# A three-layer graph convolution on one core: how many columns of each step are fetched row by row, where they land, and how SyncE and ScalarE issue them

## What is computed

```python
def _sage_conv(x, src, dst, Wl, bl, Wr):
    agg = jax.ops.segment_max(x[src], dst, num_segments=x.shape[0])
    agg = jnp.where(jnp.isfinite(agg), agg, 0.0)
    return agg @ Wl + bl + x @ Wr
h = jax.nn.leaky_relu(_sage_conv(h, src, dst, Wl1, bl1, Wr1), NEG_SLOPE)   # and twice more
x = x + h
```

## Time and profile before

| | |
|---|---|
| median of 3 runs | 6052.55 us (6050.76 to 6064.11) |
| the profiled execution, its own time | 6050.56 us |
| its span in the profile | 6048.9 us |
| GpSimd busy | 4524.8 us, 75% |
| VectorE busy | 2893.5 us, 48% |
| TensorE busy | 732.5 us, 12% |
| ScalarE busy | 225.4 us, 4% (DMA issues are not counted) |
| mean DMA rate | 180 GB/s |

### The profile page before, as it was taken

How to read it: one execution, slowest core, us unless ns; L and a number is a source line. 1 busy time by engine, 2 the same in 40 slices (tenths; PEclk the granted TensorE clock), 3 DMA queues, 4 the chain that set the end, 5 groups by cost and what they waited for, 6 DMA issues and landing times.

```text
span 6048.9 us, 53349 instructions
## 1 busy us (share of the span) xinstructions
PE 732.5 (12%) x2214; PEld 411.8 (7%) x2214; DVE 2893.5 (48%) x3638; ACT 225.4 (4%) x664; POOL 4524.8 (75%) x4793
## 2 busy tenths in 40 slices
PE   1111111111100311111111110040010000100003
PEld 0000000000000200000000000030000000000002
DVE  5333333333333555555555555565555555555556
ACT  1000000000000100000000000010000000000001
POOL 6777777777777777777777777767777777777776
PEclk7555555555555655555555555575555555555556
DMA  4333333333333566666666666666666666666665
GB/s 141 108 111 107 108 108 109 110 108 108 108 108 107 171 216 218 218 216 220 216 218 218 216 219 214 215 206 219 217 220 215 218 218 216 220 215 218 215 216 175
DMA packets 461123, 1089.10 MB, mean 180 GB/s; under 512 B 116295, under 2 KB 181740, under 8 KB 461068
## 3 DMA queue, kind: packets, MB, share of 16 engines
q0 software_dynamic: 203520, 519.10, 30.6%
q1 hardware_dynamic: 220508, 544.04, 24.8%
q10 hardware_dynamic: 37040, 25.45, 1.5%
HBM read 555.08 MB, written 533.07 MB: 180 GB/s over the span
## 4 chain that ended last, share of the span: by engine, by line
POOL 49%; issue 17%; DMA 1%; POOLq 1%; DVE 0%; PE 0%; DVEq 0%
POOL ring L448 47%; POOL ring L475 2%; POOLq L444 0%; DMA ring<-running_max_log,end_row 0%; POOLq L441 0%; DMA patch<-running_max_log,patch_row 0%; DMA ring<-features,stage 0%; DMA running_max_log<-patch 0%; POOL patch L465 0%; DVE z_sum L902 0%; DVE agg L894 0%; POOLq L455 0%; POOLq L443 0%; DMA features<-h_out 0%; DVE patch L873 0%
## 5 line engine op out<-in xcount | busy, mean ns | idle before, releaser
L448 POOL DMA_INDIRECT ring<-features,stage x4611 | 4360.0, 946 | 1432.2 <-issue 1383.7
L792 DVE TENSOR_TENSOR ring<-banks,ring 128x1024 f32<-128x1024 f32 (+1 forms) x1173 | 1227.4, 1046 | 2954.0 <-DMA ring<-features,stage 2918.9
L758 DVE TENSOR_TENSOR banks<-ring,banks 128x1024 f32<-128x1024 f32 (+1 forms) x1173 | 1232.1, 1050 | 37.5
L975 PE MATMUL banks<-wr,h_turned 128*128 128x256 f32 (+1 forms) x490 | 220.7, 596 | 3623.4 <-ACT h_turned L1109 3623.4
L975 PEld LDWEIGHTS banks<-wr,h_turned 128*128 128x128 f32 x490 | 127.2, 320 | 3687.4 <-ACT h_turned L1109 3678.6
L991 PE MATMUL banks<-dst_low,own 128*128 128x394 bf16 x200 | 100.4, 502 | 976.0 <-DVE own L734 976.0
L475 POOL DMA_INDIRECT ring<-running_max_log,end_row x147 | 142.9, 972 | 65.6 <-issue 43.9
L1109 ACT ACTIVATE h_turned<-banks 128x256 f32<-128x256 f32 (+1 forms) x147 | 51.8, 353 | 3128.6 <-issue 2664.1
L739 DVE COPY stage<-edges 128x8 int32 (+1 forms) x588 | 119.4, 203 | 88.0 <-DVE banks L758 32.8
L977 PE MATMUL banks<-b,ones 1*128 1x256 f32 (+1 forms) x294 | 157.6, 637 | 0.0
L1048 PE MATMUL banks<-wl,agg 128*128 128x256 f32 (+1 forms) x490 | 110.7, 369 | 1.2 <-DVE agg L894 0.9
(11 more groups left out here) (114 smaller groups left out, 523.4 us busy)
## 6 DMA issues: line engine op xcount, KB each, us to landing
running_max_log<-ring SPq DMA_DIRECT2D x782, 512.0 KB, 3.1
running_max_log<-ring SPq DMA_DIRECT2D x391, 256.0 KB, 2.2
ring<-features ACTq DMA_DIRECT2D x4752, 1.0 KB
ring<-features,stage POOLq DMA_INDIRECT x4611, 3.2
ring<-features SPq DMA_DIRECT2D x3888, 1.0 KB
ring<-features ACTq DMA_DIRECT2D x2376, 0.5 KB
ring<-features SPq DMA_DIRECT2D x1944, 0.5 KB
h_in<-features ACTq DMA_DIRECT2D x98, 128.0 KB, 2.5
```

The source lines that it names most:

```text
L448: pool.indirect_dma_start(ring[0:rows, c * w:(c + 1) * w], None, tables[l], bass.IndirectOffsetOnAxis(ap=stage[0:rows, b, u:u + 1].bitcast ...
L758: dve.tensor_tensor(sum_ps[:, 0:CHAINS * w].rearrange("p (h f) -> p h f", h=CHAINS), group(g - 1).rearrange("p (h f) -> p h f", h=CHAINS), ...
L792: dve.tensor_tensor(group(g), sum_ps[:, 0:CHAINS * w], group(g), ALU.max).then_inc(turn, 1)
L975: pe.matmul(mm_ps[p][:, 0:n], h_turned[p][:, c, :], wr_sb[l][:, c, :], start=(c == 0), stop=False)
```

## The change

- GpSimd gathers 54 columns a step, all of 128 rows, and none of column 54. SyncE and ScalarE fetch 128 rows each (`FETCHED_COLS` 2), into one of two buffers, `fetched[0]` and `fetched[1]`, in turn, and no longer into `ring`.
- VectorE's last maximum of a step becomes two, of half the width each: the first takes the two gathered columns from `ring`, the second the two fetched ones from `fetched`; the waits for the rows stand between them.
- Because there are two buffers, the rows of step `i` may be fetched once step `i - 2` is scanned: both queues wait for `block_scanned` of `i * BLOCKS`, and no longer for a group of the same step nor for a store.
- A TENSOR_LOAD takes 32 words (`AT_ONCE`) on both queues. SyncE does it ahead of the wait for the block, then waits, stores the whole block of 8 columns with one DMA, and issues 32 rows behind it, in blocks 0 to 3. ScalarE issues four portions of 32; in layers 1 and 2 the four pieces of `keep_pair` stand between the portions (`step_of_rows`), in layer 0 behind them all.
- The loops on VectorE, ScalarE and SyncE have a body of two steps, since the buffer must be known to the instruction; step 0 stands ahead of them. GpSimd's loop keeps a body of one step.
- The last, short step is stored group by group as before.

```diff
-SYNC_ROWS, SYNC_AT_ONCE = 72, 8
-ACT_AT_ONCE = 11
-ROWS = 160
+FETCHED_COLS = 2
+SYNC_ROWS = 128
+AT_ONCE = 32
...
+    ROWS = FETCHED_COLS * P
...
-        return width(b, last) - (b == BLOCKS - 1 and not last)
+        return width(b, last) - (FETCHED_COLS if b == BLOCKS - 1 and not last else 0)
...
+        fetched = [sb(f"fetched{k}", [P, FETCHED_COLS * F_MAX]) for k in range(2)]
...
-                            rows = 2 * P - ROWS if c == RING_COLS - 2 and not last else P
                             pool.indirect_dma_start(
-                                ring[0:rows, c * w:(c + 1) * w], None, tables[l],
+                                ring[:, c * w:(c + 1) * w], None, tables[l],
...
-                        dve.tensor_tensor(group(g), sum_ps[:, 0:CHAINS * w], group(g), ALU.max).then_inc(turn, 1)
+                        if g == GROUPS - 1:
+                            gathered = (CHAINS - FETCHED_COLS) * w
+                            dve.tensor_tensor(group(g)[:, 0:gathered], sum_ps[:, 0:gathered], group(g)[:, 0:gathered],
+                                              ALU.max).then_inc(turn, 1)
+                            dve.wait_ge(act_rows_landed[turn_of], FETCHED[1])
+                            dve.sem_inc(act_rows_landed[turn_of], -FETCHED[1])
+                            dve.wait_ge(sync_rows_landed[turn_of], FETCHED[0])
+                            dve.sem_inc(sync_rows_landed[turn_of], -FETCHED[0])
+                            dve.tensor_tensor(group(g)[:, gathered:CHAINS * w], sum_ps[:, gathered:CHAINS * w],
+                                              fetched[turn_of][:, 0:FETCHED_COLS * w], ALU.max).then_inc(turn, 1)
...
+                def rows_open(i):
+
+                    if isinstance(i, int) and i == 0:
                         act.wait_ge(rows_placed, len(widths))
                     else:
-                        act.wait_ge(logged[BLOCKS - 1], i * (DMA * STORES_OF[BLOCKS - 1]) + LOGGED[BLOCKS - 1] * l)
+                        act.wait_ge(block_scanned, i * BLOCKS + SIGNED * l)
...
+                def step_of_rows(i, pair, turn_of):
+
+                    rows_open(i)
+                    if pair and l:
+                        for p in range(2):
+                            fetch_rows(i, turn_of, range(2 * p, 2 * p + 1))
+                            keep_turned(i, p, True)
+                            fetch_rows(i, turn_of, range(2 * p + 1, 2 * p + 2))
+                            keep_own(i, p)
+                    else:
+                        fetch_rows(i, turn_of, range(ACT_PORTIONS))
+                        if pair:
+                            keep_pair(i, 2)
...
+                    elif not last:
+                        sp.wait_ge(block_scanned, i * BLOCKS + SIGNED * l)
                     for b in used_blocks(last):
 
                         c, columns = b * BLOCK_COLS, width(b, last)
-                        if columns > CHAINS:
+                        fetches = not last and b < SYNC_PORTIONS
+                        if fetches:
+                            places = row_places(0, mybir.EngineType.SP, i, b * AT_ONCE, AT_ONCE, w)
+                        if last and columns > CHAINS:
                             sp.wait_ge(group_scanned, i * BLOCKS + (FIRSTS * l + b + 1))
...
                         sp.wait_ge(block_scanned, i * BLOCKS + (SIGNED * l + BLOCKS + b + 1))
-                        at = columns - CHAINS
-                        sp.dma_start(log_block(l, i, b, at, CHAINS), ring[:, (c + at) * w:(c + columns) * w]
+                        at = columns - CHAINS if last else 0
+                        sp.dma_start(log_block(l, i, b, at, columns - at), ring[:, (c + at) * w:(c + columns) * w]
                                      ).then_inc(logged[b], DMA)
-                        if not last and (BLOCK_GROUPS * b + 1) * SYNC_AT_ONCE < SYNC_ROWS:
-                            fetch_rows(i, BLOCK_GROUPS * b + 1)
+                        if fetches:
+                            fetch_rows(places, turn_of, b * AT_ONCE)
...
-                with sp.Fori(1, STEPS - 1) as i:
-                    log_step(i, False)
+                with sp.Fori(0, STEPS // 2 - 1) as i:
+                    log_step(i * 2 + 1, False, 1)
+                    log_step(i * 2 + 2, False, 0)
```

More of the change, by code:

```diff
@@ L23 @@
 BLOCK_GROUPS = BLOCK_COLS // CHAINS
-TURNS = 2 * GROUPS + 1
+TURNS = 2 * GROUPS + 2
 STORES = 5
@@ L307, in run_neighbours, with lists_of @@
             return pairs
[L309 to L316, removed]
+        def lists_of(edges_src):
+            return [(row_list[:, k * P:(k + 1) * P],
+                     bass.AP(edges_src.tensor, (CHAINS - 1 - k) * P * RUN + GROUPS - 1, [[GROUPS, STEPS - 1], [RUN, P]]))
+                    for k in range(FETCHED_COLS)]
         def row_places(k, engine, i, at, count, w):
@@ L329, in table_row, with row_slot @@
             return tables[l].rearrange("n f -> (n f)").bitcast(U8)[bass.ds(place, 4 * w)].rearrange("(a b) -> a b", a=1)
[L331 to L336, removed]
+        def row_slot(k, turn_of, r, w):
+            ahead, p = divmod(ROWS_OF[k][0] + r, P)
+            c = FETCHED_COLS - 1 - ahead
+            return fetched[turn_of][p:p + 1, c * w:(c + 1) * w].bitcast(U8)
         block = ctx.enter_context(nc.Block())
@@ L414, in _ @@
                         pool.dma_start(dest, there).then_inc(sort_done, DMA)
-                pool.wait_ge(list_loaded, 2 * DMA)
+                pool.wait_ge(lists_and_empty, (FETCHED_COLS + len(widths)) * DMA)
                 with nc.allow_non_contiguous_dma(reason="one word of each row to fetch"):
-                    for here, there in list_of(sorted_src):
+                    for here, there in lists_of(sorted_src):
                         pool.dma_start(here, there).then_inc(sort_done, DMA)
@@ L1234, in log_step, with fetch_rows @@
-                def log_step(i, last):
+                def fetch_rows(places, turn_of, first):
+                    for r, place in enumerate(places):
+                        sp.dma_start(row_slot(0, turn_of, first + r, w), table_row(l, w, place)
+                                     ).then_inc(sync_rows_landed[turn_of], DMA)
+                def log_step(i, last, turn_of=0):
+                    if isinstance(i, int) and i == 0:
+                        sp.wait_ge(rows_placed, len(widths))
+                        if l == 0:
+                            sp.wait_ge(h0_stored, DMA * HEAD_STEPS)
+                        else:
+                            for b in range(STORES):
+                                sp.wait_ge(h_stored[b], PER_OUT * l)
+                    elif not last:
+                        sp.wait_ge(block_scanned, i * BLOCKS + SIGNED * l)
```

120 lines of the change are left out of this document (52 added, 68 removed).

## The result

The changed kernel takes 6289.9 us (median of four runs, 6284.9 to 6290.8), where the kernel before takes 6052.9 in the same comparison: 1.0386 times as long, with a 95% interval of 1.0368 to 1.0404. The forecast was 5953, faster. The range of 5940 to 6310 holds the time, but by a mechanism that none of the rivals described; that rival 2 gave 6308 is a coincidence, since its slow loads didn't occur.

A forecast was written before the change was run, and what follows sets the result against it. GpSimd's own work on gathers, 1.25 us each, was taken as the bound. Dropping one short gather in each of 81 steps takes 99 us from 6050.6, giving 5952, and 5953 for the median; range 5940 to 6310 us.

The forecast's parts named there:

- rival 2: Loads of 4.4 us in layer 0 and 5.6 in the others make ScalarE the bound: 6308 us; chance 0.15.
- GpSimd's part: GpSimd loses one short gather a step, 1.22 us: 81 steps give 99 us, new step 67.5 us.
- L: Time of a register load of 32 words on SyncE and ScalarE, taken as 2 to 3.3 us.
- Rivals 1 to 4: Slower 32-word loads make SyncE or ScalarE the bound: 6049, 6308, 7380, 6697 us; chances 0.15, 0.15, 0.03, 0.05.
- rival 4: The skill's price of about 200 ns a register makes a 32-word load 6.4 us: 6697 us; chance 0.05.
- Rival 5: Late stores make GpSimd wait; it has 49 us against 20, needing L near 12; no chance of its own given.
- ScalarE's budget: ScalarE's rows, pair work and loads: 50.2 + 4L us in layers 1 and 2, 52.9 + 4L in layer 0, against 67.5.
- SyncE's chain: SyncE's cycle from block 0's store through its rows to VectorE's last maximum: 55.6 + 3L us, over 67.5 from L = 4.0.
- With a landing of no more than the 3.1 us of a store: SyncE's last rows land within 3.1 us of issue, making 44.6 + 3L into 47.7 + 3L us.
- The stall at the back edge: Branches ending SyncE's and ScalarE's loops of some 590 instructions may stall; a few us every second step would cost little.

The follow-up runs named there:

- G2: Changed kernel with SyncE issuing only the first row of each portion, 4 of its 128 a step: 5963.0 us, 0.983 of the kernel before.
- G3: Changed kernel with ScalarE issuing only 4 of its 128 rows a step, SyncE's 128 kept: 6009.5 us, 0.991 of the kernel before.
- E2: Changed kernel with three of SyncE's four row portions issued a step ahead: 1.158 of the kernel before, at a time when that took 7850 to 7970 us.

## Why the prediction was wrong, by its own steps

**GpSimd's part: right.** 81 times one short gather, 99 us less: G2's median is 101 us under that of the kernel before. Where nothing holds GpSimd, its gathers are 1.25 us apart.

**L, on which the forecast was said to rest: right.** Loads of 32 words in layers 0 and 1 of the changed kernel (ns min/median/max), against the earlier trace rows:

```profile
L325 SPq TENSOR_LOAD <-row_at x108: 2039/2114/3237, 41.7 to 1850.5; - x108
L325 ACTq TENSOR_LOAD <-row_at x108: 2142/2230/3414, 46.5 to 1809.2; - x108
...
L325 SPq TENSOR_LOAD <-row_at x108: 2038/2112/4142, 2009.6 to 4014.0; - x108
L325 ACTq TENSOR_LOAD <-row_at x108: 2141/2193/4423, 2010.5 to 3937.8; - x108
```

2.1 to 2.2 us, the lower end of my 2 to 3.3: the slope from one word to eleven. Rivals 1 to 4 all needed 3.7 or more and fall; rival 4's 6.4 us is three times what was measured, and the measurement decides. Rival 5 falls too: GpSimd doesn't wait for stores.

**ScalarE's budget: right.** 58.6 to 59 us by the formula; ScalarE's rows and pair work run from 3082.89 to 3137.85, 55 us, and the first load of 2 to 4 us lies ahead of them. It fits in 67.5.

**SyncE's chain: this is the step that failed**, "With a landing of no more than the 3.1 us of a store". By the formula its cycle at L = 2.1 was 55.6 + 6.3 = 61.9 us. Measured are 74.1, term by term: VectorE and the start of the store 9.1 for 7.9; the issue 54.8 for 50.9, since 32 rows take 10.6 to 11.9 us and not the 10.4 of the earlier trace rows; the landing 10.2 on the average for 3.1. That is 1.2 + 3.9 + 7.1. With the first two alone the cycle would be 67.0, just under the bound; the landing decides, 6.6 us a step in 54 steps, 356 us for a measured loss of 340. The first two were too small for a case without the backlog as well: G3, with a landing of 1.5, has 69.2. The error was one of kind. I took the landing of one transfer when little is in flight as a constant, and asked of each queue alone whether it keeps up. Nobody asked what serves both queues. At 160 rows in 68.75 us that engine kept up, with no more than 12 rows waiting; by the estimate above it was occupied for 55 of 69 us. At 256 rows issued within 56 us it falls behind, and its last rows are the ones waited for.

**Layer 0** issues 256 rows too and keeps 67.5 us. There some 20 rows at most are outstanding and SyncE's last land 4 to 6 us behind their issue, more than 3.1 as well, but rows, gathers and stores are half the size, and the cycle stays inside GpSimd's.

**The stall at the back edge** was seen and priced "one of a few us every second step would cost little": 4.75 us on SyncE, and no loss while the engine is full, though in G3 it is part of the 44 us.

**Open** is how the order of E2 does where the kernel before takes 6053 us. By the traces it should help: 256 rows at 0.25 us are 64 us, and fewer at the 0.19 of the last ones, under 67.5 if they are spread over the whole step; now they can't start for the first 6 to 8 us of it. That is argued, not shown. No version that ran beats the kernel before with all its work.

## What to carry to other kernels

Before moving work from one engine to another's DMA queue, count transfers by what serves them, not only by who issues them. Small transfers of one row from two queues met on one of 16 DMA engines, and the wait appears behind the last of them, as a landing that grows with the rate. If a wait hangs on the last of many small transfers, its price is the backlog at that point: compare the rate of issue with the rate of landing, and look for a store in which one of 16 parts comes late.

## What the runs showed of the hardware that I had not expected

- One-row transfers of 1 KB from both queues together landed at 0.25 us each while they were issued at 4.6 a us, and at 0.19 once nothing more was issued; the last sixteenth of a store lands at 12.0 us behind such a backlog, and the rest by 4.4.
- A load of 32 registers from aligned words takes 2.1 to 2.2 us, 66 to 70 ns a word, less than the 2.70 and 3.01 that eleven, mostly unaligned, took by the median.
- A taken branch at the end of a loop of some 590 instructions costs SyncE 4.75 us and ScalarE 2.5, and 0.1 to 0.2 where the loop has 68 to 231.
- A transfer of one row in four pieces takes 0.58 us to issue, and one in one piece 0.23.
- The same kernel took 6053 us at one time and 7860 at another, and the issue of single rows is what grew: the 88 rows of a step in 81.7 us for 54.4. The cause is open.
